# Pairs' layers of the later quarters: three fp32r products for one fp32 product, and a smaller ring for dynamic transfers

## What is computed

```python
x = x + einsum('bct,bcd->bdt', x, W0[subject])
x = x + einsum('bct,bcd->bdt', x, W1[adapter])
x = x + einsum('bct,bcd->bdt', x, W2[adapter]) + bias[adapter][:, :, None]
gate, up = lora(x, Wg, Ag, Bg), lora(x, Wu, Au, Bu)
x = x + lora(silu(gate) * up, Wd, Ad, Bd)
# lora(x, W, A, B) = x @ W + (x @ A[adapter]) @ B[adapter]
```

## Time and profile before

| | us |
|---|---|
| median of 3 runs | 1239.54 (1239.38 to 1240.88) |
| the profiled execution | 1237.63 |
| its span | 1235.8 |

### The profile page before, as it was taken

The page is one execution under the profiler, slowest core; times in us unless marked ns, Lnnn a source line. Parts: engine busy times, 40 slices in busy tenths (PEclk is TensorE's granted clock), DMA queues, the critical chain, the costliest instruction groups (busy, mean ns, idle before and its releaser), DMA issues.

```text
span 1235.8 us, 18085 instructions
## 1 busy us (share of the span) xinstructions
PE 1227.7 (99%) x6190; PEld 1029.7 (83%) x6190; DVE 957.1 (77%) x1540; ACT 558.1 (45%) x1003; POOL 710.7 (58%) x598
## 2 busy tenths in 40 slices
PE   9999999999999999999999999999999999999998
PEld 8888888888888888888888888888888888888886
DVE  7887777887688777788678778777868877677775
ACT  4744445444544344454344444444534443444333
POOL 4676655558736556546864556555675554444453
PEclk9999999999999999999999999999999999999999
DMA  6866455556865455557496544546659442322323
GB/s 213 295 214 220 126 153 186 162 163 185 289 223 162 124 158 144 164 162 213 142 332 191 178 128 143 166 137 187 198 180 314 160 120 80 93 84 86 113 89 107
DMA packets 141690, 209.60 MB, mean 170 GB/s; under 512 B 44192, under 2 KB 88480, under 8 KB 141600
## 3 DMA queue, kind: packets, MB, share of 16 engines
q1 hardware_dynamic: 117696, 135.45, 34.8%
q0 software_dynamic: 23040, 71.85, 19.0%
q10 hardware_dynamic: 864, 1.15, 0.3%
HBM read 164.36 MB, written 44.04 MB: 169 GB/s over the span
## 4 chain that ended last, share of the span: by engine, by line
PE 97%; DVE 2%; issue 0%; ACT 0%; POOL 0%; DVEq 0%; POOLq 0%
PE px L1735 29%; PE pd L1735 28%; PE py L1735 14%; PE pz L1735 7%; PE pz L1752 3%; PE pv L1781 2%; PE pv L1779 2%; PE pd L2074 2%; PE py L1752 2%; PE px L1752 2%; PE pd L1762 1%; PE px L1886 1%; PE py L1886 1%; PE pd L1871 1%; PE px L1758 1%; PE pd L1904 0%
## 5 line engine op out<-in xcount | busy, mean ns | idle before, releaser
L803 POOL TENSOR_TENSOR h_lo<-g,h_hi 128x512 fp32r<-128x512 f32 x127 | 182.4, 1437 | 298.0 <-ACT h_hi L943 297.2
L766 POOL DMA_INDIRECT b_got<-b_table,idx_b x192 | 198.5, 1034 | 59.9 <-issue 49.9
L1735 PE MATMUL px<-xo_hi,wg_hi 128*128 128x512 f32 x516 | 207.2, 402 | 1.3 <-DVE wg_lo L1382 0.9
L1513 DVE TENSOR_TENSOR acc<-pd,acc 128x512 f32<-128x512 f32 x248 | 164.3, 684 | 51.6 <-PE pd L1735 51.6
L1382 DVE TENSOR_TENSOR wg_lo<-w_raw,wg_hi 128x512 fp32r<-128x512 f32 (+1 forms) x256 | 182.8, 720 | 26.5 <-ACT wg_hi L943 26.4
L1735 PE MATMUL px<-xo_hi,wg_lo 128*128 128x512 f32 x516 | 202.5, 392 | 0.0
L1735 PE MATMUL px<-xo_lo,wg_hi 128*128 128x512 f32 x516 | 201.0, 389 | 0.0
L943 ACT ACTIVATE wg_hi<-w_raw 128x512 fp32r<-128x512 f32 (+1 forms) x260 | 146.0, 570 | 121.1 <-PE py L1752 74.6
L1735 PE MATMUL pd<-wd_hi,h_hi 128*128 128x512 f32 x504 | 199.7, 396 | 0.0
L1735 PE MATMUL pd<-wd_lo,h_hi 128*128 128x512 f32 x504 | 197.9, 393 | 0.0
L1735 PE MATMUL pd<-wd_hi,h_lo 128*128 128x512 f32 x504 | 196.6, 390 | 0.0
(11 more groups left out here) (331 smaller groups left out, 2439.6 us busy)
## 6 DMA issues: line engine op xcount, KB each, us to landing
w_raw<-w_gu SPq DMA_DIRECT2D x65, 512.0 KB, 4.8
wd_raw<-w_dn SPq DMA_DIRECT2D x64, 256.0 KB, 3.5
xo_hi<-xops SPq DMA_DIRECT2D x21, 512.0 KB, 6.0
xo_lo<-xops SPq DMA_DIRECT2D x21, 512.0 KB, 7.3
acc<-x SPq DMA_DIRECT2D x8, 1024.0 KB, 6.8
ad_raw<-ad_table SPq DMA_DIRECT2D x16, 512.0 KB, 4.3
ad_table<-ad_rows_kept SPq DMA_DIRECT2D x12, 512.0 KB, 6.5
xops<-st_hi SPq DMA_DIRECT2D x24, 256.0 KB, 2.8
```

The lines of the kernel that those rows point to most:

```text
L766: gp.indirect_dma_start(out=dst, out_offset=None, in_=rows_of, in_offset=bass.IndirectOffsetOnAxis(ap=rows.bitcast(U32), axis=0)).then_inc ...
L803: return gp.tensor_tensor(dst, src_raw, src_hi, ALU.subtract)
L1513: ins = dve.tensor_tensor(dst, pd[j][:, :], dst, ALU.add)
L1735: ins = pe.matmul(psum, w_parts[wi], x_parts[xi], start=(start and i == 0), stop=(stop and i == 2), skip_group_check=more)
```

## The change

The product of F and x in quarters 0 to 2 becomes a split product of three fp32r terms. For that
- ScalarE makes `x_hi` (`x_high`), for pair 0 in block 3 behind `keep_s2`, for each later pair behind the `add_bias` of the pair before; the wait for the load of x moves from TensorE to it;
- GpSimd makes `x_lo` (`x_low`), in the pair's own block, behind `gather_pair`;
- VectorE adds F twice, once rounded to fp32r as `f_hi` (in columns of `v` that are free) and once to `f_one`, waits for the latter, and subtracts for `f_lo`;
- TensorE waits for `f_done` (now of `f_lo`) and `x_lo_done`.

`x_hi` and `x_lo` take 4,096 bytes of each partition. The ring that holds the descriptors of dynamic transfers is cut from 8192 to 4096 bytes.

```diff
@@ -135,6 +135,8 @@
         ea_one = sb("ea_one", [P, 2, P])
         eb_one = sb("eb_one", [P, 2, P])
         f_one = sb("f_one", [P, P])
+        x_hi = sb("x_hi", [P, T], F32R)
+        x_lo = sb("x_lo", [P, T], F32R)
         ad_raw = sb("ad_raw", [P, QS, AD_COLS])
         ad_rows_kept = sb("ad_rows_kept", [P, AD_ROWS * AD_COLS])
         ad = sb("ad", [P, 2, HALVES, 2, HC], F32R)
@@ -301,7 +303,10 @@
 
         e_got = [sem(f"e_got{i}") for i in range(2)]
         e_mm = sem("e_mm")
+        f_summed = sem("f_summed")
         f_done = sem("f_done")
+        x_hi_done = sem("x_hi_done")
+        x_lo_done = sem("x_lo_done")
         layer_mm = sem("layer_mm")
         layer_add = sem("layer_add")
 
@@ -487,6 +492,9 @@
             j = b - TURNS_FROM
             return j // 2 if q + 1 < QUARTERS and j >= 0 and j % 2 == 0 and j // 2 < TP else None
 
+        def pair_tokens(q, i):
+            return acc[:, (q + 1) % 2, PAIR_ORDER[i], :]
+
         def parts_at(q, b):
             return turn_at(q, b - 1)
 
@@ -536,6 +544,8 @@
 
         def bd_pair(q, t, j):
             return bd_of(q, t)[j // 2][0:LAST_ROWS, j % 2, :]
+
+        f_hi, f_lo = v[:, 1, WH:WH + P], v[:, 1, WH + P:2 * WH]
 
         def of_parity(ap, e):
 
@@ -851,6 +861,10 @@
                 gp.wait_ge(ad_hi_done, q * SUPER + m + 1)
                 low(ad_part(1), ad_new(m), ad_part(0)).then_inc(ad_done, 1)
 
+            def x_low(q, i):
+                gp.wait_ge(x_hi_done, made(q, i))
+                low(x_lo[:, :], pair_tokens(q, i), x_hi[:, :]).then_inc(x_lo_done, 1)
+
             def h_low(q, b, t):
                 gp.wait_ge(h_hi_done[t], blocks_done(q, b))
                 low(h_lo[:, t, b % 2, :], (g1 if t else g0)[:, :], h_hi[:, t, b % 2, :]).then_inc(h_lo_done[t], 1)
@@ -879,6 +893,8 @@
                     gp.wait_ge(idx_d_done, 1)
                 if i is not None:
                     gather_pair(q, i)
+                if pair_at(q, b) is not None:
+                    x_low(q, pair_at(q, b))
                 if b % 2:
 
                     gp.wait_ge(c11_done, k)
@@ -969,6 +985,11 @@
                 slots, _ = piece(k)
                 act.wait_ge(*piece_in(k))
                 copy(part(st_hi[:, slots, :]), st_lo[:, slots, :]).then_inc(b_hi_done, 1)
+
+            def x_high(q, i):
+                if i < 2:
+                    act.wait_ge(x_in[(q + 1) % 2][i], ((q + 1) // 2 + 1) * 16)
+                copy(x_hi[:, :], pair_tokens(q, i)).then_inc(x_hi_done, 1)
 
             def add_bias(dst, psum, pair):
                 return act.activation(dst, psum, ACT.Identity, bias=bias[:, pair:pair + 1])
@@ -1112,6 +1133,8 @@
                 if n > 1:
                     act.wait_ge(h_done[0], k - 1)
                 keep_s2(k)
+                if pair_at(q, b) == 0:
+                    x_high(q, 0)
                 if b == 1:
                     down_high(q * BLOCKS + 1)
                 if n == 3 or split and b < 2:
@@ -1172,7 +1195,9 @@
                 if i is not None:
                     pair = PAIR_ORDER[i]
                     act.wait_ge(layer_mm, made(q, i))
-                    add_bias(acc[:, (q + 1) % 2, pair, :], pd[0][:, :], (q + 1) * QP + pair).then_inc(layer_add, 1)
+                    add_bias(pair_tokens(q, i), pd[0][:, :], (q + 1) * QP + pair).then_inc(layer_add, 1)
+                    if i + 1 < QP:
+                        x_high(q, i + 1)
 
                 def keep_c21():
                     act.wait_ge(p4_mm, k)
@@ -1674,8 +1699,11 @@
                     dve.wait_ge(e_mm, e)
                     if e > 1:
                         dve.wait_ge(layer_mm, e - 1)
+                    dve.tensor_tensor(f_hi, pd[2][:, 0:P], eb_one[:, i % 2, :], ALU.add)
                     dve.tensor_tensor(f_one[:, :], pd[2][:, 0:P], eb_one[:, i % 2, :], ALU.add
-                                      ).then_inc(f_done, 1)
+                                      ).then_inc(f_summed, 1)
+                    dve.wait_ge(f_summed, e)
+                    dve.tensor_tensor(f_lo, f_one[:, :], f_hi, ALU.subtract).then_inc(f_done, 1)
                 if to_own:
                     own_difference(q + 1)
                 c11(k)
@@ -2068,11 +2096,10 @@
 
                     lora11()
                 if i is not None:
-                    if i < 2:
-                        pe.wait_ge(x_in[(q + 1) % 2][i], ((q + 1) // 2 + 1) * 16)
                     pe.wait_ge(f_done, made(q, i))
-                    pe.matmul(pd[0][:, :], f_one[:, :], acc[:, (q + 1) % 2, PAIR_ORDER[i], :],
-                              start=True, stop=True).then_inc(layer_mm, 1)
+                    pe.wait_ge(x_lo_done, made(q, i))
+                    split_product(pd[0][:, :], [f_hi, f_lo], [x_hi[:, :], x_lo[:, :]]
+                                  ).then_inc(layer_mm, 1)
                 if b == 0:
                     if q:
                         pe.wait_ge(y_add, (q - 1) * QP + TP)
@@ -2193,7 +2220,7 @@
     arrays.update({f"ad_rows{g}": ad_rows[g].reshape(-1, AD_ROWS * AD_COLS) for g in range(AD_GROUPS)})
     arrays = {name: np.ascontiguousarray(v) for name, v in arrays.items()}
 
-    nc = bacc.Bacc("TRN2", target_bir_lowering=False, num_devices=1, dynamic_dma_scratch_size=8192)
+    nc = bacc.Bacc("TRN2", target_bir_lowering=False, num_devices=1, dynamic_dma_scratch_size=4096)
     t = {name: nc.dram_tensor(name, v.shape, mybir.dt.from_np(v.dtype), kind="ExternalInput").ap()
          for name, v in arrays.items()}
     out = nc.dram_tensor("out", (SAMPLES, C, T), F32, kind="ExternalOutput").ap()
```

## The result

| | before | changed |
|---|---|---|
| median, us | 1239.55 (4 runs, 1239.38 to 1240.88) | 1259.85 (4 runs, 1256.89 to 1262.26) |
| profiled execution, us | 1237.63 | 1260.59 |
| its span, us | 1235.8 | 1258.5 |
| its mean granted clock | 1.000 | 0.997 |

The ratio is 1.016, 95% interval 1.0148 to 1.0172: 1.6% slower. The forecast was 1256 in a range of 1247 to 1266: 16.5 us slower, where the medians show 20.3.

A forecast was written before the change was run, and what follows sets the result against it. TensorE, busy 99% of the span, was taken as the bound, with new waits paid in full. Waits of 21.0 us less 4.1 gained make 16.9, taken as 16.5 slower: 1239.54 becomes 1256, range 1247 to 1266.

The forecast's parts named there:

- The bound: Whole kernel: TensorE is busy 99% of the span, so any new wait of it is added in full.
- The sum: All places: 21.0 us of waits less 4.1 us of gain, 16.9 us slower, taken as 16.5.
- the port: VectorE and GpSimd sharing SBUF: 3.5 us at block 10, 1.5 us for x_low late behind wg_lo at five places.
- The product: At 24 places three fp32r terms replace one fp32 product: 0.17 us less each, 4.1 us in all.
- The queue of GpSimd: Blocks 4, 6 and 8: x_low behind the gathers makes TensorE wait at nine places, 15.7 us in all.
- Odd blocks: Gathers end early there, so x_low is ready in time: cost 0 at 12 places, with one exception.
- Block 3 of quarter 0: x_high(0) waits for the load of x; 0.3 us taken, 2.2 if the first load is the slow one.
- f_lo's delay: VectorE's added sums make f_done 0.6 to 0.7 us later; covered by x_lo's wait in blocks 4, 6, 8: cost 0.
- the rival on odd blocks: Blocks 5, 7 and 9: VectorE loses the port there too, some 0.7 us at 9 places, 6 us: 1262; 8%.
- The clock: Rival: TensorE's clock falls at the four waits above 2.3 us, up to 11.6 us more, 1268; 5%.
- The ring: Smaller descriptor ring: cost 0, no gather waits for a place; rival that it throttles gathers, 1299, 3%.
- The other side: Rival: at the edited product the inputs arrive in time and only the gain is left, 1235.4; 7%.

The follow-up runs named there:

- experiment 2: Also called x_low_early: the changed kernel with GpSimd's x_low of each later pair moved one block earlier, ahead of h_low(b, 0); 1235.89 us, ratio 0.9963.
- 4: The changed kernel with x_low put ahead of gather_pair in the same block instead of behind it; 1247.95 us, ratio 1.0060.
- experiment 8: The kernel before, fp32 product kept, with x_high and x_low run at the changed kernel's places and their results unused; 1242.96 us, ratio 1.0016.
- Experiments 5 to 7: experiment 2 with x_low back in its own block: block 8, 1246.12 us; block 8 done twice, 1255.10; blocks 4 and 6 except quarter 0's block 4, 1242.93.
- experiment 1: The kernel before with only the ring cut from 8192 to 4096 bytes; 1240.83 us, ratio 1.0001.

## Why the prediction was right, and where its terms were off

**The bound.** TensorE was the bound and every new wait came through in full: the product of the last place is late by the sum of the table above, and no later step swallowed a wait.

**The sum.** It came out nearer than its terms, which is in part luck: the port was priced 2.2 us too high (3.5 and 1.5 against 2.8), while the low clock (3.2) and the dearer first terms behind a wait (1.1) stood in no term.

**The product.** Forecast 0.17 us each and 4.1 in all; measured 0.18 (experiment 2), 4.3. The rule of four passes for fp32 (the Trainium skill, FP8 and Floating Point Precision, TensorE Precision Notes) agrees with the 0.86 us, 3.7 times the 0.233 of one fp32r term; the passes themselves no run shows. The 215.7 ns for a product of 512 columns of the Trainium skill (TensorE: Matmul & The Clock Gate, Wait — 56ns, not 53.3ns?) would give 5.1 (24 x (0.86 - 0.647), an estimate), and no run here shows it: the chain shows 0.70 for three fp32r terms, 0.233 each, and 4.3.

**The queue of GpSimd.** The nine waits were forecast at 15.7 us by adding the gather's end, 1.30 and 0.14. They came out as 5.2 + 3.6 + 7.1 = 15.9. That the queue is the cause is shown by experiment 2, where the same subtraction elsewhere leaves none of them, and 4. Odd blocks cost nothing, as forecast, but not with the slack that was forecast (see the port). Block 3 of quarter 0 waited 0.46 us (0.3 forecast) and 1.0 in experiment 2.

**The port.** Block 10 was forecast at 3.5 us from the held sums of the earlier trace rows, and took 2.8. The Trainium skill (SBUF — State Buffer, SBUF: two separate sides) has the port as an exclusive lock, held for a whole instruction; the 3.42 us of L1516 agree. The mechanism needs a correction: I let VectorE's waiting sum get in between h_lo and x_lo. It did not get in; GpSimd's next subtraction followed at once. VectorE was so held once and not twice, and f_lo ended 4.97 us after the start of h_lo (242.00 - 237.03) where the forecast had 5.14. The 1.5 us for x_low starting late behind wg_lo did not come: in block 8 x_lo started at the gather's end and wg_lo (201.71) was the one that waited. But in block 6, where I had put f_lo's delay under the wait for x_lo, f_lo lost the port and ended the wait 0.15 us after x_lo.

In the odd blocks the port took more than I had counted, and that none of it was paid was luck. Block 9 of quarter 0 has:

```profile
218.29 2.16 DVE L1391 TENSOR_TENSOR w_raw<-w_raw 128x256 f32<-128x256 f32 x1
...
222.36 0.29 DVE L1706 TENSOR_TENSOR v<-f_one,v 128x128 fp32r<-128x128 f32 x1
```

x_lo (218.86 to 220.16) holds the second sum of weights for 2.16 us, and f_lo ends at 222.65, some 0.05 us ahead of the product at 222.70, which is as close as where TensorE waits for it. In quarters 1 and 2 it was 0.16 and 0.13, where the rival on odd blocks had counted a slack of 0.7 to 1.0. In experiment 8, where x_low came 0.26 us earlier against the product, it held the first of these sums instead, and that cost 0.7 us at each block 9.

**The clock.** This was a rival at 5%, priced at up to 2.9 us for each wait above 2.3 us. It took place, in part: behind two of the four waits of that length, at about 1.6 us each. The sum left it out, and this is the largest term that was missing: 3.2 us in the profiled execution. Windows of 1 us around the first fall, behind the wait that ended at 122.74:

```profile
123.00:124.00 1.00, 1.00 (x6) 1.00 0.00 0
124.00:125.00 1.00, 1.00 (x4) 0.60 0.27 102
125.00:126.00 1.00, 1.00 (x5) 0.50 1.01 379
126.00:127.00 1.00, 1.00 (x6) 0.50 0.12 43
127.00:128.00 1.00, 1.00 (x4) 0.69 0.00 0
128.00:129.00 1.00, 1.00 (x8) 1.00 0.00 0
```

The granted clock goes from full (2.4 GHz) to half (1.2 GHz) 1.5 us after the products have resumed, for some 3.4 us, and costs about 1.6. It fell for as long at block 8 of quarter 1, there 0.2 us before the product started, and not at block 8 of quarters 0 and 2 with the same wait; why not, no run shows. Experiments 5 to 7 tie the falls to the longer waits, in the profiled executions: none behind waits of 1.2 to 1.3 us, behind 2 of 3 at 2.4, behind 3 of 3 at 4.1. It fits that the changed kernel's four executions spread over 5.4 us, with mean clocks of 0.998, 0.997, 0.997 and 0.994 from the quickest to the slowest. My argument against it, that a pause of 0.9 us had left the clock alone, was from a pause too short to bear on it. And the slow first products of the earlier trace rows were no case of it: the granted clock reads full there.

**The ring.** No cost, as forecast (experiment 1: ratio 1.0001).

**The other side.** The rival by which all inputs arrive in time was wrong for this order of the queues and right for another: 1235.4 was its price, and x_low_early measured 1235.9.

## What to carry to other kernels

When a helper's operation is added to an engine that is 58% busy, its share says nothing; look up at each place what the engine does right then, and put the operation where the engine waits, as soon as its inputs are there, not next to its consumer. Where the bound engine has no waits, a new one of 1 us is paid in full, and one of 2 us or more may be paid again in clock. A trade of 0.18 us per product is worth making only if the operands cost no wait at all: here the same edit was 1.6% slower or 0.4% faster by the place of one statement.

## What the runs showed of the hardware

- TensorE's clock was halved for some 3.4 us at 4 of 7 pauses of 2.2 to 2.4 us in the midst of dense work, and at all three of 3.9 us (once for 6.8 us), at 1.5 to 2.7 us each; at pauses of the edited product of up to 1.1 us (all by the idle time in the records) never. The fall began from 1.1 us before the products resumed to 1.5 us after.
- Among the small products at the program's start it fell for 3.4 us right behind pauses of 1.35, 1.66 and 1.86 us in three of the ten profiled executions, and not behind one of 1.64; eight 512-column records then took 5.37 us instead of 3.67.
- GpSimd's second subtraction in a row went ahead of a VectorE operation that had been waiting for the port: 3.42 us for a sum of 128x256 that takes 0.42.
- The first fp32r term behind a wait took 0.30 us to the next start instead of 0.23.
- One profiled execution's start was 2 to 3 us quicker than the others' (first large product at 29.0 against 30.9 to 31.7 where the clock didn't fall), with and without the change.
